# Layer-norm rows and context rows normalised by GpSimd, epsilon added by VectorE, both query halves written by one instruction, and a new stream order, in a four-block transformer kernel

## What is computed

```
mu = jnp.mean(x, axis=-1, keepdims=True)
var = jnp.var(x, axis=-1, keepdims=True)
return (x - mu) * jax.lax.rsqrt(var + EPS)
...
attn = jnp.einsum('bhnd,bhsd->bhns', q, k) * SCALE
attn = jax.nn.softmax(attn, axis=-1)
o = jnp.einsum('bhns,bhsd->bhnd', attn, v)
```

## Time and profile before

| what | value |
|---|---|
| executions timed | 1738.8, 1743.8, 1744.63 us; median 1743.8 us |
| span of the profiled execution, first to last instruction | 1743.3 us, 83583 instructions |
| busy: TensorE matmuls (PE) | 1645.2 us, 94% |
| busy: TensorE weight loads (PEld) | 1392.3 us, 80% |
| busy: VectorE (DVE) | 1420.7 us, 81% |
| busy: ScalarE (ACT) | 1467.5 us, 84% |
| busy: GpSimd (POOL) | 891.4 us, 51% |
| granted TensorE clock, mean | 0.992 of full speed |

### The profile page before, as it was taken

How to read it: one execution, slowest core, us unless ns; L and a number is a source line. 1 busy time by engine, 2 the same in 40 slices (tenths; PEclk the granted TensorE clock), 3 DMA queues, 4 the chain that set the end, 5 groups by cost and what they waited for, 6 DMA issues and landing times.

```text
span 1743.3 us, 83583 instructions
## 1 busy us (share of the span) xinstructions
PE 1645.2 (94%) x35621; PEld 1392.3 (80%) x35621; DVE 1420.7 (81%) x3824; ACT 1467.5 (84%) x3585; POOL 891.4 (51%) x1881
## 2 busy tenths in 40 slices
PE   5987999999999999999999999999999999999998
PEld 4766788888878888788888888788888877877887
DVE  5877888988888898788888888788888888898764
ACT  3676888898898888898898989888898888788886
POOL 5434554555555455555455555545555555555442
PEclk9999999999999999999999999999999999999999
DMA  7000000000000000000000001000000100000000
GB/s 234 3 15 9 18 25 24 9 24 21 21 25 25 24 9 24 18 25 24 24 15 19 18 24 24 24 3 24 25 24 24 25 15 19 18 15 16 3 6 16
DMA packets 57821, 41.80 MB, mean 24 GB/s; under 512 B 13552, under 2 KB 56176, under 8 KB 57328
## 3 DMA queue, kind: packets, MB, share of 16 engines
q1 hardware_dynamic: 57456, 36.46, 7.3%
HBM read 31.99 MB, written 4.46 MB: 21 GB/s over the span
## 4 chain that ended last, share of the span: by engine, by line
PE 76%; DVE 10%; ACT 7%; issue 3%; DMA 1%; POOL 1%; SPq 1%; ACTq 0%; DVEq 0%; POOLq 0%
PE half L1088 10%; PE half L965 9%; PE half L992 8%; PE half L1007 8%; PE half L1033 6%; PE half L1023 6%; PE half L1097 5%; PE half L838 5%; PE half L1016 4%; DVE top L1251 4%; PE half L952 4%; PE half L937 3%; PE half L941 3%; PE half L987 3%; ACT pT L1478 1%
## 5 line engine op out<-in xcount | busy, mean ns | idle before, releaser
L1251 DVE TENSOR_REDUCE top<-half 128x32 f32<-128x2048 f32 x160 | 366.0, 2287 | 56.3 <-PE half L965 54.5
L1443 ACT ACTIVATE pT<-half 128x512 f32<-128x512 f32 x640 | 329.7, 605 | 56.3 <-PE half L992 54.7
L1478 ACT ACTIVATE pT<-half,mod 128x64 f32<-128x64 f32 x896 | 195.1, 343 | 17.6 <-PE half L1088 16.5
L965 PE MATMUL half<-k_heads,q_heads 32*128 32x128 f32 x5120 | 191.6, 284 | 15.5 <-issue 8.4
L965 PEld LDWEIGHTS half<-k_heads,q_heads 32*128 32x128 f32 x5120 | 162.2, 187 | 42.0 <-issue 22.2
L778 POOL TENSOR_TENSOR rstd<-shifted,minus_halves 128x2 f32<-128x2 f32 x256 | 183.0, 715 | 20.0
L992 PE MATMUL half<-q_heads,k_heads 32*128 32x128 f32 x5120 | 184.0, 279 | 6.9 <-issue 6.9
L776 POOL TENSOR_TENSOR shifted<-moments,eps 128x2 f32<-128x2 f32 x256 | 51.6, 201 | 267.8 <-DVE moments L1212 266.8
L806 POOL TENSOR_TENSOR top<-top 128x32 f32<-128x32 f32 x160 | 39.4, 246 | 289.1 <-DVE top L1251 288.5
L1007 PE MATMUL half<-pT,v_cols 128*32 128x64 f32 x10240 | 177.8, 221 | 7.4 <-issue 5.6
L1007 PEld LDWEIGHTS half<-pT,v_cols 128*32 128x32 f32 x10240 | 153.3, 110 | 36.5 <-issue 25.2
(11 more groups left out here) (154 smaller groups left out, 3926.3 us busy)
## 6 DMA issues: line engine op xcount, KB each, us to landing
gates<-gate_store SPq DMA_DIRECT2D x128, 128.0 KB, 3.3
x_rows<-x SPq DMA_DIRECT2D x32, 128.0 KB, 2.7
c_rows<-context SPq DMA_DIRECT2D x32, 128.0 KB, 2.4
out<-n_rows SPq DMA_DIRECT2D x32, 128.0 KB, 1.9
w_sb<-weights SPq DMA_DIRECT2D x1, 1856.0 KB, 7.3
w_sb<-weights SPq DMA_DIRECT2D x2, 512.0 KB, 6.3
logit_bias<-logit_store SPq DMA_DIRECT2D x64, 1.5 KB, 3.5
row_sb<-rows SPq DMA_DIRECT2D x1, 769.5 KB, 8.5
```

Source lines behind the costliest of these rows:

```text
L965: mm = nc.tensor.matmul(halves[HALF_OF[n]][:, g, tb * D:(tb + 1) * D], q_heads[s][part, tb, :, :], k_heads[s][part, tb, :, :], start=True, ...
L1251: nc.vector.tensor_reduce(term[s][0], halves[HALF_OF[n]][:, :, :].rearrange("p g (c k) -> p g c k", k=SEQ), AX.X, ALU.max).then_inc(tops_r ...
L1443: nc.scalar.activation(turn_cols[s][:, g, :], halves[HALF_OF[n]][:, g, :], ACT.Exp, scale=ATT_SCALE).then_inc(scores_read, 1)
L1478: m = nc.scalar.activation(dst, src[:, at], ACT.Silu, bias=mod[s][:, k, tb:tb + 1])
```

## The change

1. Epsilon: the step `eps` follows moments, and `c_eps` follows c_moments. VectorE adds epsilon there as an immediate (one instruction for x, two for the context), after waiting for its own `bn_aggr`. GpSimd keeps the power. The tensor `eps`, `minus` and `c_minus` are gone.
2. Normalising: at step normal GpSimd, not ScalarE, normalises tile 1 of x, by a `tensor_scalar` that subtracts the mean and multiplies by `rstd`. The context's two tiles are normalised by GpSimd too, in a step of their own, `c_normal`, that stands just ahead of the out or fc2 before the `kvnorm`; it waits for `c_rstd` and for ScalarE to have taken out the last result that was computed from `nT`.
3. Queries: `q_heads` is laid out with the two halves interleaved, and one `scalar_tensor_tensor` of 512 elements writes both, in place of two `tensor_scalar` of 256. The matmuls of step scores read `low` and `q_heads` with a step of two elements.
4. TensorE: tops waits for k before q; values for the exponentials first, then v, then the bank; `l3_experts` for the hidden values before the bank.
5. `SEQUENCE` is a new string, of 4626 characters in place of 4274 (11 steps more in each of the 32 groups: 8 `eps`, 1 `c_eps`, 2 `c_normal`). `HALVES` is the same.

```diff
+EPS = [1e-5, 1e-6]
...
 def moments(eps):
-    return [("stats", eps), ("moments", eps)]
+    return [("stats", eps), ("moments", eps), ("eps", eps)]
...
-    [("load", None), *moments(TIGHT), ("normal", None), ("context", None), ("c_moments", None)]
+    [("load", None), *moments(TIGHT), ("normal", None), ("context", None), ("c_moments", None), ("c_eps", None)]
...
+def with_context_norms(steps):
+
+    out = list(steps)
+    for i in reversed(range(len(steps))):
+        if steps[i][0] == "kvnorm":
+            at = max(m for m in range(i) if steps[m][0] in ("out", "fc2"))
+            out.insert(at, ("c_normal", steps[i][1][0]))
+    return out
+
+
+GROUP_STEPS = with_context_norms(GROUP_STEPS)
...
 SEQUENCE = (
...
 )
...
-    m = next_step(next_step(n))
+    m = next_step(next_step(next_step(n)))
     return ORDER[m][1] if ORDER[m][0] == "kvnorm" else None
...
-CONTEXT_NORMS = {n: next_kv(n)[0] for n, (kind, _, _) in enumerate(ORDER) if kind == "stats" and next_kv(n)}
...
-CONTEXT_NORMS_EACH = len(CONTEXT_NORMS) // GROUPS
+CONTEXT_NORMS_EACH = sum(kind == "c_normal" for kind, _ in GROUP_STEPS)
...
+def last_read(n):
+
+    return max(m for m in range(n) if ORDER[m][2] == ORDER[n][2] and ORDER[m][0] in ("fc1", "v"))
...
-        eps = sb("eps", [D, 2, 2])
...
-        minus = each("minus", [D, 1])
-        c_shifted, c_rstd, c_minus = each("c_shifted", [D, 2, 2]), each("c_rstd", [D, 2, 2]), each("c_minus", [D, 2, 2])
+        c_shifted, c_rstd = each("c_shifted", [D, 2, 2]), each("c_rstd", [D, 2, 2])
...
-        q_heads, k_heads = each("q_heads", [D, GROUP, 2, SEQ]), each("k_heads", [D, GROUP, 2, SEQ])
+        q_heads, k_heads = each("q_heads", [D, GROUP, SEQ, 2]), each("k_heads", [D, GROUP, 2, SEQ])
...
-        weighed = [q[:, :, :, :].rearrange("p g l q -> p (g l q)") for q in q_heads]
+        weighed = [q[:, :, :, :].rearrange("p g q l -> p (g q l)") for q in q_heads]
...
-        b2_part = [q[:, :, :, :].rearrange("p (e t) l q -> p e t (l q)", e=2) for q in q_heads]
+        b2_part = [q[:, :, :, :].rearrange("p (e t) q l -> p e t (q l)", e=2) for q in q_heads]
...
-                nc.gpsimd.memset(eps[:, LOOSE, :], 1e-5).then_inc(consts_made, 1)
-                nc.gpsimd.memset(eps[:, TIGHT, :], 1e-6).then_inc(consts_made, 1)
                 nc.gpsimd.memset(minus_halves[:, :, :], -0.5).then_inc(consts_made, 1)
...
                 for n, (kind, arg, s) in enumerate(ORDER):
-                    if kind == "c_moments":
+                    if kind == "c_eps":
                         count.next(c_moments_in)
-                        variances = c_moments[s][:, :, 1].unsqueeze(1).broadcast_to([D, 2, 2])
-                        means = c_moments[s][:, :, 0].unsqueeze(1).broadcast_to([D, 2, 2])
-                        nc.gpsimd.tensor_tensor(c_shifted[s][:, :, :], variances, eps[:, :, :], ALU.add).then_inc(pool_own, 1)
-                        count.next(pool_own)
-                        nc.gpsimd.tensor_tensor(c_rstd[s][:, :, :], c_shifted[s][:, :, :], minus_halves[:, :, :], ALU.pow).then_inc(pool_own, 1)
-                        count.next(pool_own)
-                        nc.gpsimd.tensor_tensor(c_minus[s][:, :, :], means, c_rstd[s][:, :, :], ALU.mult).then_inc(pool_own, 1)
-                        count.next(pool_own)
-                        nc.gpsimd.tensor_scalar(c_minus[s][:, :, :], c_minus[s][:, :, :], -1.0, None, ALU.mult).then_inc(c_scaled[s], 1)
-                    if kind == "moments":
+                        nc.gpsimd.tensor_tensor(c_rstd[s][:, :, :], c_shifted[s][:, :, :], minus_halves[:, :, :], ALU.pow).then_inc(c_rstd_in[s], 1)
+
+                    if kind == "c_normal":
+
+                        pool.wait_ge(c_rstd_in[s], round_of(n) + 1)
+                        pool.wait_ge(a_emptied, freed_by(last_read(n), FOR_SCALAR))
+                        for t in range(2):
+                            m = nc.gpsimd.tensor_scalar(cn_rows[s][:, t, :], c_rows[s][:, t, :], c_moments[s][:, t, 0:1], c_rstd[s][:, arg, t:t + 1],
+                                                        ALU.subtract, ALU.mult)
+                        m.then_inc(c_normed[s], 1)
+
+                    if kind == "eps":
                         count.next(moments_in)
-                        nc.gpsimd.tensor_tensor(shifted[s][:, :], moments[s][:, :, 1], eps[:, arg, :], ALU.add).then_inc(pool_own, 1)
-                        count.next(pool_own)
                         nc.gpsimd.tensor_tensor(rstd[s][:, :], shifted[s][:, :], minus_halves[:, 0, :], ALU.pow).then_inc(rstd_in[s], 1)
+
+                    if kind == "normal":
                         count.next(rstd_in[s])
-                        nc.gpsimd.tensor_scalar(minus[s][:, :], moments[s][:, 1, 0:1], -1.0, rstd[s][:, 1:2], ALU.mult, ALU.mult).then_inc(minus_in[s], 1)
+                        nc.gpsimd.tensor_scalar(n_rows[s][:, 1, :], x_rows[s][:, 1, :], moments[s][:, 1, 0:1], rstd[s][:, 1:2],
+                                                ALU.subtract, ALU.mult).then_inc(rows_normed[s], 1)
+
                     if kind == "q" or kind == "fc1" and arg[1] == 0:
 
                         pool.wait_ge(*x_changed(n))
...
                     if kind == "tops":
 
+                        after("k", s)
                         after("q", s)
-                        after("k", s)
                         wait_emptied(pe, HELD_BEFORE[n], emptied)
...
                         for tb in range(GROUP):
                             for g in range(TURNS):
                                 part = slice(32 * g, 32 * g + 32)
-                                nc.tensor.matmul(halves[HALF_OF[n]][:, g, tb * D:(tb + 1) * D], of_keys[part, 2 * tb:2 * tb + 2, :], low[s][part, :],
+                                nc.tensor.matmul(halves[HALF_OF[n]][:, g, tb * D:(tb + 1) * D], of_keys[part, 2 * tb:2 * tb + 2, :],
+                                                 low[s][part, :].rearrange("p (q l) -> p l q", l=2),
                                                  start=tb == 0, stop=False)
                         for tb in range(GROUP):
                             for g in range(TURNS):
                                 part = slice(32 * g, 32 * g + 32)
-                                mm = nc.tensor.matmul(halves[HALF_OF[n]][:, g, tb * D:(tb + 1) * D], k_heads[s][part, tb, :, :], q_heads[s][part, tb, :, :],
+                                mm = nc.tensor.matmul(halves[HALF_OF[n]][:, g, tb * D:(tb + 1) * D], k_heads[s][part, tb, :, :], q_heads[s][part, tb, :, :].rearrange("p q l -> p l q"),
                                                       start=False, stop=tb == GROUP - 1)
                                 if tb == GROUP - 1:
                                     mm.then_inc(scores_filled, 1)
...
                     if kind == "values":
 
+                        after("pT", s)
                         after("v", s)
                         dst = to_v.slot()[:, :].rearrange("p (b h l q) -> p b h l q", b=GROUP, h=2, l=2)
-                        after("pT", s)
                         for tb in range(GROUP):
...
                     if kind == "l3_experts" and arg < EXPERTS:
+                        pe.wait_ge(*ready["hidden", s, arg])
                         dst, e = to_v.slot(), arg
-                        pe.wait_ge(*ready["hidden", s, e])
                         for t in range(2):
...
                         after("c_stats", s)
                         for t in range(2):
                             m = nc.vector.bn_aggr(c_moments[s][:, t, :], c_stats[s][:, t, :])
+                        makes("c_moments", s, m)
...
+
+                    if kind == "c_eps":
+                        after("c_moments", s)
+                        for e in (LOOSE, TIGHT):
+                            m = nc.vector.tensor_scalar(c_shifted[s][:, e, :], c_moments[s][:, :, 1], EPS[e], None, ALU.add)
                         m.then_inc(c_moments_in, 1)
...
                         after("stats", s)
                         for t in range(2):
                             m = nc.vector.bn_aggr(moments[s][:, t, :], stats[s][:, t, :])
-                        m.then_inc(moments_in, 1)
+                        makes("moments", s, m)
+
+                    if kind == "eps":
+                        after("moments", s)
+                        nc.vector.tensor_scalar(shifted[s][:, :], moments[s][:, :, 1], EPS[arg], None, ALU.add).then_inc(moments_in, 1)
...
                     if kind == "q":
 
                         src = banks.take()
-                        for lo in range(2):
-                            m = nc.vector.tensor_scalar(q_heads[s][:, :, lo, :], bank4(src), bias(*arg["bq"]), own_head[:, 2 + lo:3 + lo],
-                                                        ALU.add, ALU.mult)
-                        m.then_inc(v_emptied, 1)
+                        nc.vector.scalar_tensor_tensor(out=q_heads[s][:, :, :, :].rearrange("p g q l -> p (g q) l"),
```

(51 more changed lines are left out.)

64 lines of the change are left out of this document (19 added, 45 removed).

## The result

The changed kernel takes 1757.8 us (median of five, 1751.97 to 1763.41) against 1744.6 for the one before: a ratio of 1.0082, 95% interval 1.0063 to 1.0102. The same kernel in a later set of runs gave 1.0091 (1.0074 to 1.0108). It is slower, where the forecast was 1728 us and faster. The profiled execution took 1757.35 us, its span is 1755.6. Its granted TensorE clock is 0.996 of full speed in the mean, against 0.992 before, so the clock is no cause of the loss.

What follows compares the result with a forecast made beforehand. TensorE's matmuls fill 1645.2 of 1743.3 us, so gains come from 98.1 us of idle time in many short waits. Sum: 1743.3 - 16 (order) + 0 = 1727, with 0.5 us of the median 1728 us; range 1703 to 1760.

Steps and rivals of the forecast that it cites:

- a collision with VectorE: Layer norm halves on VectorE and GpSimd start together and block each other at SBUF: 1757 us, chance 0.15.
- the price of GpSimd's instruction: GpSimd's new 128x128 normalising instruction: 0.42 us each, 384 of them 161 us, with 109 and 286 as ends.
- The wait that hung on it: Layer norms held in GpSimd's queue and c_normal's wait for ScalarE: put at nothing while the order leaves room.
- The order's term: New step order fills TensorE's idle time after 45 us: four tenths of a 39 us bound, -16 us.
- the weaker stretches: TensorE's idle time outside the best stretch, 300 to 900 us; most gain expected in 45 to 300 and after 900.
- The epsilons and queries: VectorE: merged query instruction saves 45 us, 320 epsilon instructions add 50; together +5 us, counted as nothing.
- 183 us: ScalarE sheds 256 normalisations and 128 of the context, 183.2 us, falling to about 1284; none on the path by itself.
- the stepped reading: TensorE reads q_heads and low with a step of two: taken as 0, bounds 141 and 70 us.
- the reordered waits: TensorE's waits in a new order change nothing in what is awaited; taken as 0.
- The first rival: VectorE becomes the later engine: halves at 0.60 us, VectorE at 1526 us, total 1757 us; chance 0.15.
- The third rival: Nothing gained: ScalarE's work was hidden, GpSimd's queue holds layer norms behind splits as long; 1743 us, chance 0.14.

Runs made afterwards that it cites:

- a2_one_op: Changed kernel, but GpSimd's instruction on tile 1 only subtracts the mean, without multiplying by rstd (output not the reference's): 0.9991 of the kernel before, 1744.25 us.
- a4_short: Changed kernel, but GpSimd sets tile 1 to zero twice instead of normalising it (0.42 us, work left out): 0.9934 of the kernel before, 1734.7 us.
- b2_q_one: Kernel before and its order, with only the single 512-element query instruction and the stepped reading of q_heads and low: ratio 0.9951, 1738.6 us.
- a9_q_two: Changed kernel and its order, but queries written by two instructions in the old layout: 1.0173 of the kernel before, 1775.7 us.
- a7_c_scalar: Changed kernel and its order, but ScalarE normalises the context's rows at step c_normal and GpSimd makes c_minus: 1.0085 of the kernel before, 1762.3 us.
- a1_x_scalar: Changed kernel and its order, but ScalarE normalises tile 1 of x again, GpSimd making minus behind the power: 1.0705 of the kernel before, 1869.8 us.
- b4_waits: Kernel before with only the order of TensorE's waits changed as in the diff: ratio 0.9987, 1744.2 us.
- a6_both_vector: Changed kernel and its order, but VectorE normalises both tiles of x: 1.0097 of the kernel before, 1763.3 us.
- b8_all_old: All parts of the change in the order of the kernel before, with eps, c_eps and c_normal steps inserted: 1.0502 of the kernel before, 1835.0 us.
- b1_x_pool: Kernel before and its old order, with only tile 1 of x normalised by GpSimd, minus and ScalarE's instruction gone: ratio 1.0363, 1809.0 us.

## Why the prediction was wrong

The measured 1757.8 us lies in the range (1703 to 1760), but on the side to which 0.21 had been given. That it lies in the range at all is luck: the upper end stood there for a collision with VectorE that did not come.

- **The step that failed is the price of GpSimd's instruction**, "I take 0.42", with 0.28 to 0.74 around it. It measured 0.840 and 0.819 us, 318 us in place of 161. The upper end came from a row with two tensors read and one operation per element; the new instruction reads one tensor but does two operations. a2_one_op shows that the second operation is worth 0.20 us of the 0.42 by which the price was off. The other 0.22 is there with one operation too (0.64 us), and no run shows where it comes from.
- **The wait that hung on it was put at nothing.** The sum, 1743.3 - 16 + 0, has no term for TensorE behind GpSimd, so even the upper end of 0.74 us would not have moved it. The new waits on GpSimd were taken as free "as long as the order leaves room", and the second tile was to come sooner. It came later (0.59 us behind the first in the median, against 0.20), in GpSimd's strictly ordered queue it came behind other streams' tiles, and TensorE waited 32.8 us for it. At 0.42 us this wait is still 11.8 us.
- **The order's term** was -16 us. With the length as priced, a4_short gives 0.66%, 11.5 us, so the forecast's sign comes out and its size nearly so, and the 25 us or so between a4_short and the changed kernel are the instruction's length. But those 11.5 us are the whole change's and not the order's alone. The one query instruction, which the prediction booked as "nothing" together with the epsilons, is worth 0.5% by itself in the old order (b2_q_one) and 0.8% in the new one (a9_q_two), 9 to 14 us. What is left of the 11.5 us for ScalarE's relief, the order and the other parts together is, by these figures, at most 3. Against the old order under the new division the new string is worth 4%: it pays for most of what the division costs. That the freed ScalarE lets the order fill the weaker stretches, the mechanism of the forecast, is not shown.
- **The epsilons and queries** as "+5, nothing" of VectorE's time were right in busy time (+7.3 us; the epsilons of x took 206 ns each in place of 155) and wrong in effect: in the old order the epsilons cost 12 us and the queries gave 9; in the new one, taking either back made the kernel slower.
- **ScalarE's** 183 us turned out as 154. The groups of its lines add up to 1554 us before and 1369 after, 186 less, but the page counts the time once in which instructions of two groups overlap, and 87 us of such overlap before are 55 after. That the context's part was off the path by itself is shown by a7_c_scalar, where 47 us come back and the time stays. For the 127 us of the tiles of x no run shows it: a1_x_scalar brings them back together with the wait for `minus`.
- **TensorE**: the stepped reading cost nothing (277 ns against 279, 184.3 us in all against 184.0), the reordered waits nothing (b4_waits, 0.9987), as taken. The rule of the Trainium skill on 16-byte lines ("SBUF — State Buffer", note on cachelines), by which a step of two float32 keeps full bandwidth, agrees.
- **The first rival** named 1757 us, and for the wrong reason. Its sign, VectorE's halves at 0.60 us and VectorE over 1500 us, did not come: they take 368 ns in the mean against 370 before, and VectorE is at 1428. That the two engines block each other, which the prediction took from the Trainium skill ("Advanced Engine Details and Errata", VectorE Performance Modes), does not show in VectorE's mean. GpSimd's instruction has 790 ns at least, 802 in the median and 1195 at most; whether VectorE is what stretches its longest ones is not shown.
- **The third rival** came nearest in mechanism. The sign that was named for it is there: TensorE's idle time stays near 98 us (107.6) with more of it behind GpSimd, 32.8 us behind the new tile. The timeline at 1480 us shows tiles held in GpSimd's queue, but behind each other; how much stood behind the splits, as the rival had it, is not separated, and the instruction's length was not part of it.

## What to carry to other kernels

When an operation moves to an engine that has no row for it, a row with other operations does not bound its price from above, even one that reads more operands and twice the elements: here the 0.74 us of such a row lay under the 0.84 measured. Give the wait behind the new instruction a term of its own in the sum, and ask what the forecast becomes at the upper end. An order written for one division of work belongs to it: of seven moves of one part to another engine in a given order, five cost 0.7 to 6% and two made no difference (a6_both_vector, a7_c_scalar), with idle time on every engine, so the division and the order can only be judged together. An engine that is 61% busy can still be the one that sets the end, if its queue is strict and what it makes is awaited at once.

## What the runs showed that was not expected

- GpSimd's `tensor_scalar` on 128 x 128 float32 takes 0.64 us with one operation and 0.84 with two; setting the same tile to zero 0.21 us; two tensors of 256 elements with one operation 0.74.
- TensorE's busy time is not a constant of the program: the same 35621 matmuls read as 1643.9 us in b2_q_one and as this in a1_x_scalar:

```profile
PE 1684.3 (90%) x35621; PEld 1415.4 (76%) x35621; DVE 1428.5 (76%) x3984; ACT 1417.3 (76%) x3455; POOL 923.5 (49%) x1655
```

  Most of the difference goes with the granted clock: 0.976 of full speed in the mean in a1_x_scalar, 0.993 in b2_q_one, which over their spans is 45 and 12 us of full-speed time, a difference of 33 where the busy times differ by 40. Here are 64 matmuls of L1028 in a1_x_scalar in a stretch at a granted clock of 0.50 (1.2 GHz) and 64 more in one at 1.00 (2.4 GHz); ns at least, in the median and at most:

```profile
L1028 PE MATMUL half<-pT,v_cols x64: 311/311/317, 564.4 to 566.0; 128*32 128x64 f32 x64
L1028 PE MATMUL half<-pT,v_cols x64: 219/219/243, 169.2 to 170.1; 128*32 128x64 f32 x64
```

  What makes up the rest is not shown. The three kernels in which TensorE stands still longest have the lowest means of all (with a1_x_scalar, b8_all_old at 0.981 and b1_x_pool at 0.985), so the 98.1 us of idle time that the prediction took as the ceiling of any gain understate what waits cost: a1_x_scalar is 112 us slower than the changed kernel with 76 us more idle.
